# Causal mask of the max pieces: from a fused VectorE add-and-maximum to a TensorE product of identity and mask

## What is computed

```python
att1 = jnp.einsum('bhqd,bhkd->bhqk', q1, k1) * scale      # 16 heads, head size 16
att2 = jnp.einsum('bhqd,bhkd->bhqk', q2, k2) * scale
att1 = jax.nn.softmax(jnp.where(mask, att1, neg), axis=-1)   # mask: lower triangle, neg: -inf
att2 = jax.nn.softmax(jnp.where(mask, att2, neg), axis=-1)
att = att1 - lam[None] * att2
y = jnp.einsum('bhqk,bhkd->bhqd', att, v)
...
x = _layernorm(x + _L0_attn_ref(x, ...), axis=-1)
x = _layernorm(x + _L0_ffn_ref(x, ...), axis=-1)
```

## Time and profile before

| | |
|---|---|
| median of 3 runs | 6630.94 us (6627.46 to 6631.82) |
| the profiled execution | 6624.44 us, span 6622.7 us |
| mean granted TensorE clock | 0.974 |
| TensorE matmul busy | 6136.3 us, 93% |
| VectorE busy | 4122.0 us, 62% |
| ScalarE busy | 3503.0 us, 53% |
| GpSimd busy | 838.8 us, 13% |

### The profile page before, as it was taken

How to read it: one execution, slowest core, us unless ns; L and a number is a source line. 1 busy time by engine, 2 the same in 40 slices (tenths; PEclk the granted TensorE clock), 3 DMA queues, 4 the chain that set the end, 5 groups by cost and what they waited for, 6 DMA issues and landing times.

```text
span 6622.7 us, 98310 instructions
## 1 busy us (share of the span) xinstructions
PE 6136.3 (93%) x34048; PEld 2590.7 (39%) x34048; DVE 4122.0 (62%) x10780; ACT 3503.0 (53%) x6980; POOL 838.8 (13%) x1937
## 2 busy tenths in 40 slices
PE   8999999999999999997899999999999999999985
PEld 3333333333333333322444444444444444444431
DVE  5776767666766766674565565565655655556543
ACT  4665656566665656554445545455445454554532
POOL 2222222222222222221000000000000000000000
PEclk9999999999999999999899999999999999999997
DMA  3223232232323223232000000000000000000004
GB/s 65 46 46 58 47 57 46 46 59 43 60 48 56 49 47 54 46 55 76 4 14 10 10 14 7 13 10 10 17 20 14 13 7 13 10 10 13 7 10 152
DMA packets 136939, 229.08 MB, mean 35 GB/s; under 512 B 40476, under 2 KB 40604, under 8 KB 135680
## 3 DMA queue, kind: packets, MB, share of 16 engines
q1 hardware_dynamic: 136448, 222.83, 16.4%
HBM read 53.86 MB, written 33.55 MB: 13 GB/s over the span
## 4 chain that ended last, share of the span: by engine, by line
PE 70%; DVE 12%; ACT 10%; issue 7%; DMA 2%; SPq 1%; DVEq 0%; POOL 0%; POOLq 0%; ACTq 0%
PE ps L660 13%; PE ps L731 10%; PE ps L625 7%; PE ps L855 6%; PE ps L644 5%; PE ps L880 4%; ACT pt L1040 4%; PE ps L782 4%; PE ps L821 4%; PE ps L551 3%; PE ps L802 2%; DVE wy L1355 2%; PE ps L790 2%; PE ps L562 2%; DVE junk L1330 2%
## 5 line engine op out<-in xcount | busy, mean ns | idle before, releaser
L1040 ACT ACTIVATE pt<-ps 128x1024 f32<-128x1024 f32 (+7 forms) x2048 | 1219.3, 648 | 941.8 <-PE ps L644 940.7
L1330 DVE CUSTOM_DVE_ANT_0 junk<-ps,causal 128x128 bf16<-128x128 f32 (+3 forms) x2048 | 989.1, 486 | 540.7 <-PE ps L625 535.1
L660 PE MATMUL ps<-pt,vs 128*32 128x512 f32 (+3 forms) x6144 | 1244.6, 498 | 0.5 <-POOL pt L1702 0.2
L660 PE MATMUL ps<-pt,ones 128*32 128x512 f32 (+3 forms) x6144 | 1244.9, 498 | 0.0
L625 PE MATMUL ps<-kt,qt 96*128 96x512 bf16 (+3 forms) x3072 | 1018.2, 333 | 98.6 <-DVE mc L1330 73.6
L1334 DVE TENSOR_REDUCE mc<-ps 128x1 f32<-128x512 f32 x1024 | 704.2, 688 | 330.8 <-PE ps L625 316.9
L644 PE MATMUL ps<-qt,kt 98*128 98x512 bf16 (+3 forms) x3072 | 756.9, 328 | 30.9 <-ACT pt L1040 30.2
L731 PE MATMUL ps<-wqkv,xs 128*128 128x512 f32 x1536 | 738.6, 614 | 13.9 <-DMA wqkv<-in_wqkv 13.9
L625 PEld LDWEIGHTS ps<-kt,qt 96*128 96x128 bf16 x3072 | 296.2, 96 | 1154.0 <-DVE mc L1330 778.5
L1702 POOL TENSOR_SCALAR_AFFINE_SELECT pt<-pt 128x256 f32<-128x256 f32 x1024 | 447.0, 437 | 2285.7 <-ACT pt L1040 2285.7
L1150 ACT ACTIVATE sm<-sm,mxw 128x256 f32<-128x256 f32 (+1 forms) x1024 | 497.2, 487 | 428.0 <-DVE mxw L1501 427.6
(11 more groups left out here) (147 smaller groups left out, 7987.5 us busy)
## 6 DMA issues: line engine op xcount, KB each, us to landing
qt<-part SPq DMA_DIRECT2D x768, 64.0 KB, 2.4
kt<-part SPq DMA_DIRECT2D x768, 64.0 KB, 2.6
ya<-wy SPq DMA_DIRECT2D x128, 128.0 KB, 2.3
yb<-wy SPq DMA_DIRECT2D x128, 128.0 KB, 2.3
xs<-between_phases SPq DMA_DIRECT2D x32, 512.0 KB, 3.8
between_phases<-xo SPq DMA_DIRECT2D x32, 512.0 KB, 2.8
xt<-in_x SPq DMA_DIRECT2D x16, 512.0 KB, 5.7
between_phases<-xt SPq DMA_DIRECT2D x16, 512.0 KB, 2.8
```

Of the source, the lines that this page charges most:

```text
L660: mmi = pe.matmul(ps[32 * q:32 * q + 32, 4 + half, lo - half * 512:hi - half * 512], w, pt[:, kb % 2, i, lo:hi], start=kb == 0, stop=kb == ...
L1040: act.activation(pt[:, kb % 2, i, kb * P:1024], ps[:, 2 * i:2 * i + 2, :].rearrange("p a q -> p (a q)")[:, kb * P:1024], ACT.Exp, scale=SC ...
L1330: ins = dve.tensor_tensor_reduce(out=junk[:, bank - 6, 0:w], in0=ps[:, bank, 0:w], in1=causal[:, 512 - w:512], scale=1.0, scalar=NEG, op0= ...
```

## The change

Each diagonal piece gets a second matmul on TensorE, with the 128 by 128 identity in bf16 as its stationary side and a 128 by 128 bf16 mask `causal_b` as its moving side. It accumulates onto the last 128 columns of the piece, and the signal `max_full` moves from the first matmul to this one. DVE takes every piece with `reduce_max`; the fused operation, its accumulator read, the tile `junk` and the wait that guarded it go. `causal` shrinks from 512 to 128 columns. DVE makes `causal_b` from it at the start, after the chain on the `lam` inputs, and TensorE's first instruction waits for that. -3e38 plus a score stays far below every allowed score, so the maxima are the same but for rounding of the constant.

```diff
-        causal = sb("causal", [P, 512], F32)
+        causal = sb("causal", [P, P], F32)
+        causal_b = sb("causal_b", [P, P], BF16)
...
-        junk = sb("junk", [P, 2, 512], BF16)
...
-            pe.wait_ge(const_ready, done(8))
-            pe.wait_ge(ident_ready, done(1))
+            pe.wait_ge(const_ready, done(7))
+            pe.wait_ge(ident_ready, done(2))
...
             def piece(g, k, slot):
-                r, c0, w, _ = PIECES[k % 12]
+                r, c0, w, diag = PIECES[k % 12]
...
-                pe.matmul(ps[:, bank_of(slot), 0:w], qt[0:KDIM, u, i, r * P:(r + 1) * P],
-                          kt[0:KDIM, u, i, c0:c0 + w], start=True, stop=True).then_inc(max_full, 1)
+                mmi = pe.matmul(ps[:, bank_of(slot), 0:w], qt[0:KDIM, u, i, r * P:(r + 1) * P],
+                                kt[0:KDIM, u, i, c0:c0 + w], start=True, stop=not diag)
+                if diag:
+                    mmi = pe.matmul(ps[:, bank_of(slot), w - P:w], ident_b[:], causal_b[:], start=False, stop=True)
+                mmi.then_inc(max_full, 1)
...
             dve.wait_ge(lam_ready, done(8))
-            dve.wait_ge(const_ready, done(8))
+            dve.wait_ge(const_ready, done(7))
+            dve.tensor_copy(causal_b[:], causal[:]).then_inc(ident_ready, 1)
...
-                into = mc[:, i, c0 // 512, r:r + 1]
-                if diag:
-                    if slot >= 2:
-                        dve.wait_ge(max_free, done(slot - 1))
-                    ins = dve.tensor_tensor_reduce(out=junk[:, bank - 6, 0:w], in0=ps[:, bank, 0:w],
-                                                   in1=causal[:, 512 - w:512], scale=1.0, scalar=NEG,
-                                                   op0=ALU.add, op1=ALU.max, accum_out=into)
-                else:
-                    ins = dve.reduce_max(into, ps[:, bank, 0:w], AX_X)
-                ins.then_inc(max_free, 1)
+                dve.reduce_max(mc[:, i, c0 // 512, r:r + 1], ps[:, bank, 0:w], AX_X).then_inc(max_free, 1)
...
-            pool.memset(junk[:], 0.0).then_inc(const_ready, 1)
-            pool.wait_ge(const_ready, done(7))
-
-            pool.affine_select(out=causal[:], in_=causal[:], compare_op=ALU.is_ge, fill=NEG, base=512 - P,
-                               pattern=[[-1, 512]], channel_multiplier=1).then_inc(const_ready, 1)
+            pool.wait_ge(const_ready, done(6))
+
+            pool.affine_select(out=causal[:], in_=causal[:], compare_op=ALU.is_ge, fill=NEG, base=0,
+                               pattern=[[-1, P]], channel_multiplier=1).then_inc(const_ready, 1)
```

More of the change, by code:

```diff
@@ L993, in _ @@
             act.wait_ge(w_ready, sent(TENSORS_A))
-            act.wait_ge(const_ready, done(8))
+            act.wait_ge(const_ready, done(7))
             act.wait_ge(lam_ready, done(1))
@@ L1320, in piece @@
             def piece(g, k, slot):
-                r, c0, w, diag = PIECES[k % 12]
+                r, c0, w, _ = PIECES[k % 12]
                 i, bank = k // 12, bank_of(slot)
```

## The result

| | before | changed |
|---|---|---|
| median | 6629.28 us (6627.46 to 6631.82, 4 runs) | 6722.82 us (6719.81 to 6725.11, 4 runs) |
| ratio | 1 | 1.0141, 95% interval 1.0123 to 1.0158 |
| the profiled execution | 6624.44 us, span 6622.7 us | 6724.92 us, span 6723.2 us |
| TensorE matmul busy | 6136.3 us | 6272.4 us |
| VectorE busy | 4122.0 us | 4113.9 us |

The changed kernel is 93.5 us slower. The forecast was 80 us slower, and the time lies in the stated range of 6684 to 6765 us. DVE's busy time of the whole kernel fell by 8 us only, where the prediction had it fall by about 168 us, the sum of the accumulator reads: the recorded spans of the other operations overlap the reads, so their time was never busy time of its own.

A forecast was written before the change was run, and what follows sets the result against it. TensorE was taken as the bound except at a few waits for DVE or ACT. 77.5 us for 126 groups, 0.5 for groups 0 and 1 and 2.0 at the start make 80 us on 6630.9: 6711 us, range 6684 to 6765.

The forecast's parts named there:

- What bounds the kernel: First phase: TensorE busy 2459 of 2580 us, its chain stepping over to DVE or ACT at a few places.
- Wait A: TensorE's wait ahead of piece 9, 0.43 us, for DVE, which took piece 7 only after the 1.2 us normalisation.
- The added matmul: 16 a group on TensorE, 2048 in all, each costing 0.057 us: 0.91 us a group.
- rival 1: Identity's load not hidden, or accumulation waits for columns just written: 0.16 us a matmul, 6857 us; chance 0.10.
- What is hidden: Added matmuls inside an existing TensorE wait cost nothing: 76 of 256, or 4.75 a group.
- C: TensorE's wait behind piece 0, 0.43 us, for ACT's long exponential; hides added matmuls of pieces 23 and 0.
- D: TensorE's 0.33 us wait ahead of piece 21, where DVE has its share of a projection or output after piece 18.
- DVE's part: Plain maximum releases its bank 0.01 us sooner; three releases lie on waits: 0.025 us a group gained.
- The start: TensorE's first matmul at 15.25 instead of 13.26, as it now also waits for `causal_b`: 2.0 us later.
- 11.25 x 0.057 = 0.64 us a group on the path: Cost on TensorE of the added matmuls left after 4.75 of 16 a group are hidden.
- that new load is hidden: Behind a 128 wide bf16 piece, the next matmul with new fp32 weights starts 0.06 us later, without a gap.

## Why the prediction came out right, and which term was mis-sized

- **What bounds the kernel.** Right: TensorE, with a few waits at fixed places. Wait A removed in three of four heads gave 0.445 us in each such group, and no new one opened. Removed in the others too, it did open a new one, where DVE had two long operations in a row: piece 12 then started 0.9 us later.
- **The added matmul, 0.057 us.** Right: 0.056 (two products in a group, 0.111 to 0.115 us) to 0.059. The step named the load of the identity as the one unknown; it is hidden, and the accumulation waits for nothing, so rival 1 falls. Ahead of the 32 column products the next start is 0.15 us behind the product, as it was behind a 128 wide piece: the turn is paid once, with or without the product. The Trainium skill, page "TensorE: Matmul & The Clock Gate", section "Back-to-back issue gap", gives about 81 ns for a load and matmul of 128 columns in a sustained stream. The traces do not agree: product behind product it is 0.059 us.
- **What is hidden.** The mechanism was right, by direct test. A fell from 0.43 to 0.37, C from 0.43 to 0.30 and D from 0.33 to 0.26. One count was wrong: head 12 was given six hidden products, but its group grew by 0.85 us, just as those of heads 10 and 11 did, which were given three.
- **DVE's part, 0.025 us a group.** Right: 0.021 and 0.022.
- **The start, 2.0 us.** Right in sum, 15.28 against 13.26, with two errors of about 0.25 us that cancel.
- **The mis-sized term** is "11.25 x 0.057 = 0.64 us a group on the path". It took every successor of an added matmul to be as well covered as before. The text said of the fp32 load behind a 128 wide piece that "that new load is hidden", from the start of one matmul. That one does start on time; the next is 0.052 late, and the merged rows of the kernel before already told it, 1.05 against 1.11 us for the same eight matmuls. In groups with a projection it is 0.10 to 0.12 us. In 77 of the 110 groups whose length was compared no wait took it back, and on the mean of all 110 it makes 0.076 us, of the 0.118 that the forecast lacked.
- **The rest** is small. In 23 of the 110 groups the normalisation takes 1.32 instead of 1.21 us, and these groups are 0.11 longer: 0.02 on the mean. It leaves 0.02 us. More than half of it (0.012) is head 12 with its wrong count. What then remains is within 0.001 us steps of the product's price, 0.058 or 0.059 in place of 0.057, and wasn't tested by itself.

The sum for the whole, from the two profiled executions, which are 100.5 us apart: TensorE starts 2.0 us later, the pieces ahead of the first transpose add 0.5, all groups between first and last transpose add 94.9, and what follows the last transpose 3.1. That last part runs the same instructions in both kernels and differs by as much among the other traces, so it is scatter. The 97.4 us ahead of it and the 93.5 between the medians stand against the 80 of the forecast.

## What to carry to other kernels

Before moving work from one engine to another, ask what the work costs where it is: 16 accumulator reads of 82 ns, recorded under the next operation's span, were worth 0.02 us a group all together, while their replacement on the engine that bounds the kernel cost 0.058 us each. Count the pieces that fall inside existing waits, for these are free, and remember that they stop being free once somebody removes the wait. What a short matmul fails to cover can show two matmuls later, so compare the whole run behind it and not just the next start.

## What the runs showed that was not expected

- A 128 wide matmul ahead of a run with fp32 weights delays the run's second matmul, not its first: 1.11 us for eight instead of 1.05.
- In the changed kernel, in the changed kernel with the moved normalisation, and in the one with product and fused operation both, 24 of the 128 normalisations took 1.32 us (1.31 in the last) instead of 1.21; in the other kernels none did. The changed kernel, all of them and then one, with what GpSimd did at the time:

```profile
L1350 DVE TENSOR_TENSOR wy<-ev,rb x128: 1206/1207/1320, 122.1 to 3178.7; 64x1024 f32<-64x1024 f32 x128
```

```profile
696.44 0.41 POOL L1696 TENSOR_SCALAR_AFFINE_SELECT pt<-pt 128x256 f32<-128x256 f32 x1 [2.89 <-ACT pt L1043]
```

```profile
696.61 1.31 DVE L1350 TENSOR_TENSOR wy<-ev,rb 64x1024 f32<-64x1024 f32 x1
```

  All 72 slow ones begin while GpSimd's zeroing of the diagonal block still has 0.23 to 0.25 us to run. None of the others does: in the traces of all twelve kernels the zeroing has at most about 0.04 us left when they begin, or begins after them, or does not meet them. Where it begins just after them, within 0.1 us, it is GpSimd that is held up, with 1.40 us instead of 0.41, and the normalisation keeps its 1.21. So the two operations get in each other's way, and the added products slow the normalisation only by moving it to where the zeroing is under way. No kernel moved one of the two on purpose, so this rests on how they go together in the traces.
